# Graph network on one core: GpSimd's join to X moved into the second cell pass, biases added by one matmul per PSUM bank

## Time and profile before

| | us |
|---|---|
| median of 3 runs | 10096.06 |
| lowest, highest | 10090.6, 10096.87 |
| the profiled execution: its time | 10127.15 |
| its span, first to last instruction | 10125.4 |
| POOL busy in the span, share | 49% |
| PE, DVE, ACT busy | 55%, 52%, 46% |

### The profile page before, as it was taken

One profiled execution on the slowest core, in us unless ns is written; L12 is line 12 of the kernel. 1 busy time (PEld: TensorE's weight loads), 2 busy tenths in 40 slices (PEclk: granted clock), 3 DMA queues, 4 the chain that ended last, 5 costly groups with the idle time before them and its releaser, 6 DMA issues.

```text
span 10125.4 us, 129123 instructions
## 1 busy us (share of the span) xinstructions
PE 5609.1 (55%) x33883; PEld 4488.5 (44%) x33883; DVE 5300.4 (52%) x12476; ACT 4632.1 (46%) x8410; POOL 4936.4 (49%) x5153
## 2 busy tenths in 40 slices
PE   3999899734544545444455545544434444444446
PEld 2777666524444444443444444444423333333334
DVE  5888611335555555554555555555634444444445
ACT  2555300245555555553555555555434444444444
POOL 1000100356666666662566666666466666666660
PEclk9999899755555555555555555555555555555557
DMA  2333355134433434332344434443322222222221
GB/s 83 139 140 140 128 190 190 36 101 102 107 102 102 102 102 104 105 103 61 94 103 107 103 101 103 103 107 102 81 71 70 76 71 70 75 71 70 71 75 33
DMA packets 600502, 985.17 MB, mean 97 GB/s; under 512 B 330887, under 2 KB 454493, under 8 KB 560781
## 3 DMA queue, kind: packets, MB, share of 16 engines
q1 hardware_dynamic: 216924, 540.94, 16.1%
q0 software_dynamic: 163376, 356.21, 15.4%
q10 hardware_dynamic: 219648, 81.82, 3.0%
HBM read 755.78 MB, written 222.74 MB: 97 GB/s over the span
## 4 chain that ended last, share of the span: by engine, by line
PE 32%; DVE 21%; another core or an unknown queue 17%; DVEq 15%; issue 12%; ACT 1%; POOL 1%; POOLq 1%; DMA 0%; ACTq 0%; SPq 0%
PE bank L1038 12%; DVEq L1352 12%; DVE acc L1982 10%; PE bank L1264 9%; DVE arena L1969 3%; PE bank L1192 2%; PE bank L1062 2%; PE bank L1204 2%; DVEq L1982 2%; DVE bank L1938 2%; DVE arena L1940 1%; DVEq L1974 1%; DVE x_mem L1628 1%; PE bank L1174 1%
## 5 line engine op out<-in xcount | busy, mean ns | idle before, releaser
L704 POOL DMA_INDIRECT arena<-row_table,staged_idx x4980 | 4700.9, 944 | 3090.9 <-issue 1750.2
L1264 PE MATMUL bank<-arena 128*128 128x136 f32 x9984 | 2491.5, 430 | 1535.2 <-DVE acc L1982 739.9
L1264 PEld LDWEIGHTS bank<-arena 128*128 128x128 f32 x9984 | 2206.2, 317 | 1707.3 <-issue 1684.6
L1982 DVE TENSOR_TENSOR acc<-acc,bank 128x136 f32 x4992 | 1476.5, 296 | 2126.1 <-issue 822.6
L861 ACT ACTIVATE pick_dist<-col,dst_local 128x128 bf16<-128x128 f32 x4992 | 1521.8, 388 | 562.8 <-remote 492.0
L1038 PE MATMUL bank<-arena 128*128 128x385 bf16 (+1 forms) x7448 | 1324.8, 327 | 37.4 <-DVE arena L1722 20.9
L813 ACT COPY x_mem<-bank 128x384 f32<-128x384 f32 x416 | 198.9, 478 | 1813.1 <-remote 1159.1
L1038 PEld LDWEIGHTS bank<-arena 128*128 128x128 bf16 x7448 | 701.9, 98 | 458.5 <-issue 21.3
L648 POOL TENSOR_TENSOR arena<-acc,node_stat 128x896 f32 x14 | 23.9, 1709 | 1675.0 <-POOLq L660 988.0
L1969 DVE TENSOR_TENSOR arena<-arena,bank 128x528 f32<-128x528 f32 x1248 | 832.1, 687 | 0.7
L1204 PE MATMUL bank<-ident,x_mem 96*128 96x96 f32 x1664 | 364.7, 374 | 741.9 <-DVE x_mem L1630 574.4
(11 more groups left out here) (371 smaller groups left out, 5507.7 us busy)
## 6 DMA issues: line engine op xcount, KB each, us to landing
arena<-dst_rows SPq DMA_DIRECT2D x156, 1024.0 KB
cell_rows<-arena SPq DMA_DIRECT2D x75, 1568.0 KB, 5.1
arena<-cell_rows SPq DMA_DIRECT2D x75, 1568.0 KB, 6.6
edge_stats<-x_mem ACTq DMA_DIRECT2D x416, 192.0 KB
arena<-row_table,staged_idx POOLq DMA_INDIRECT x4980
x_mem<-in_edge_attr SPq DMA_DIRECT2D x208, 192.0 KB
x_mem<-segment_flags SPq DMA_DIRECT2D x416, 96.0 KB
arena<-change_rows SPq DMA_DIRECT2D x312, 64.0 KB
```

The source lines that it names most:

```text
L704: pool.indirect_dma_start(gathered[:, at, :], None, table, bass.IndirectOffsetOnAxis(staged_idx[:, at:at + 1], 0)).then_inc(att_gathered[n ...
L1264: mm = pe.matmul(region(k)[:, 0:ROW], pick[:, k, :], gathered[:, b * GROUP + k, :], start=True, stop=True)
L1982: done = dve.tensor_tensor(row, row, region(m * BATCH + k), ALU.add)
```

## The change

Two edits. On GpSimd, the additions of the parts of Hp and of gn_bias to X leave the loop with `scale_sums` and become a loop of their own, ahead of it, which waits only for d1.folded to be 2; the loop of `scale_sums` then waits for the end of the pass, as before. On PE, the bias matmul per tile becomes one matmul per PSUM bank with the bias broadcast over the tiles of that bank (512 and 384 columns for layer 1; 420, 420 and 140 for a table), and the accumulation is closed at the last tile of a bank.

```diff
             pool.memset(acc[:, :], 0.0).then_inc(n1.cleared, 1)
-            pool.wait_ge(d1.added, CG + 2)
-            pool.sem_inc(n2.turned, FREE)
+            pool.wait_ge(d1.folded, 2)
             with pool.Fori(0, NTG) as i:
-                scale_sums(n2, i)
-
                 x_group = X[:, bass.ds(i * TG, TG), :]
                 for m in range(PARTS):
                     pool.tensor_tensor(x_group, x_group, Hp[:, bass.ds(i * TG, TG), m * D:(m + 1) * D], ALU.add)
                     pool.drain()
                 pool.tensor_tensor(x_group, x_group, norm_par[:, 1, :].unsqueeze(1).to_broadcast([P, TG, D]),
                                    ALU.add).then_inc(n2.joined, 1)
+
+            pool.wait_ge(d1.added, CG + 2)
+            pool.sem_inc(n2.turned, FREE)
+            with pool.Fori(0, NTG) as i:
+                scale_sums(n2, i)
...
+                if bias is not None:
+                    for first in range(0, TG, 4):
+                        n = min(4, TG - first)
+                        pe.matmul(bank[:, 4 + first // 4, 0:n * P].rearrange("p (t w) -> p t w", w=P), part_ones[:, :],
+                                  bias.unsqueeze(1).to_broadcast([PARTS, n, P]), start=True, stop=False)
                 for t in range(TG):
-                    if bias is not None:
-                        pe.matmul(cols(4, t), part_ones[:, :], bias, start=True, stop=False)
                     pe.matmul(cols(4, t), own[:, t, :], w_own, start=bias is None, stop=False)
-                    mm = pe.matmul(cols(4, t), mean[:, t, :], w_mean, start=False, stop=True)
+                    mm = pe.matmul(cols(4, t), mean[:, t, :], w_mean, start=False,
+                                   stop=bias is None or t % 4 == 3 or t == TG - 1)
...
+                for first in range(0, TG, 3):
+                    tiles = min(3, TG - first)
+                    pe.matmul(bank[:, 2 + 3 * (i % 2) + first // 3, 0:tiles * TW].rearrange("p (t w) -> p t w", w=TW),
+                              part_ones[:, :], tab_bias[:, n, :].unsqueeze(1).to_broadcast([PARTS, tiles, TW]),
+                              start=True, stop=False)
                 for t in range(TG):
-                    pe.matmul(table_cols(i, t), part_ones[:, :], tab_bias[:, n, :], start=True, stop=False)
-                    mm = pe.matmul(table_cols(i, t), turned_own[i % 2][:, t, :], w_tab[:, n, :], start=False, stop=True)
+                    mm = pe.matmul(table_cols(i, t), turned_own[i % 2][:, t, :], w_tab[:, n, :], start=False,
+                                   stop=t % 3 == 2 or t == TG - 1)
```

## The result

The changed kernel takes 10032.44 us (median of 4 runs, 10027.24 to 10041.2), the kernel before on the same chip 10094.72 us (4 runs, 10090.6 to 10096.87). The ratio is 0.9945, 95% interval 0.9933 to 0.9957: 55 us by the ratio (43 to 68 by the interval), 62 us between the medians. Forecast were 10041 us and 55.5 us. In a second series on another chip the ratio was 0.9947 (0.9934 to 0.9961).

The account below looks back on a forecast made before the run. TensorE was taken to bound the second cell pass, GpSimd the product stage. Terms 31 + 7.5 + 15 + 10 - 8 = 55.5 us, off the median of 10096.06, gave 10041 us; range 10017 to 10074.

Parts of the forecast that it names:

- Join leaves the product stage: Layer 1's product stage: GpSimd's round shrinks to one multiplication, TensorE's idle 6.26 us goes; 31 us together with the bias.
- Bias, product stage: Layer 1's products: one bias matmul per bank saves net 2.0 us per group at full clock, within the stage's 31 us.
- Tables, first stage: First table stage: the first and last two product groups are on the path, 2.5 us each; gain 7.5 us.
- Tables, second stage: Second table stage: rounds fall from 8.45 to 6.50 us, then set by VectorE with ACT; gain 15 us.
- Tables, third stage: Third table stage: same code, with an unexplained 10.00 us ACT wait kept; gain 10 us, between 2.5 and 15.
- swallowed: Behind the table stages: if the "issue" wait ends at its own time, 32.5 us don't arrive; 10073 us, chance 0.11.
- Join in the pass: Start of the second pass: VectorE's small drained steps wait for GpSimd's moved join, the fold is late; loss 8 us.
- Let through: Start of the second pass: only VectorE steps with two SBUF inputs wait, fold in time; loss 0, 10033 us, chance 0.15.
- Starved: Start of the second pass: VectorE waits per instruction (10058 us) or until GpSimd's 28 are through (10083); chance 0.12.
- slower by the clock: Second pass: the new pause lowers TensorE's clock, 8.0 us per group; slower than before from seven groups; chance 0.05.

Follow-up runs that it names:

- late_join: Changed kernel, but GpSimd's join to X waits for VectorE's second fold (d1.folded 4 instead of 2); 10077.47 us, ratio 0.9940 to the kernel before.
- short_join: Changed kernel with each of GpSimd's 21 additions of Hp's parts cut in three; 10090.23 us in one run, kernel before 10148.3.
- pertile128: Kernel before with bias operands on 128 rows, still per tile, and the join to X behind VectorE's second fold; 10058.89 us, ratio 0.9938.
- rows128: Kernel before with bias operands on 128 rows instead of 3, zeros added; 10106.51 us in one run, later timed at 10084.08, ratio 0.9963.
- late128_tail: late_join with 128-row bias operands, the last 14 edge-sum gathers and their joining moved late into the third attention layer; 10051.72 us, ratio 0.9932 to before.

## Why the prediction was right, and where it wasn't

- **Join leaves the product stage**: right. Alone 17.2 us, with the bias 31.5; the next limit is TensorE with gelu, the round 6.40 us (6.15 said). The hit of half a us on the stage is partly luck: six rounds were 1.5 us longer in sum than said, and the last products, left wholly at the lower clock in the sum, fell to it only for a part of their time and were 1.6 us faster than that. In late_join, short_join and pertile128 they ran at full clock.
- **Bias, product stage**: the size was right, 1.8 us a group (2.0 said; 8.19 less 6.40), and the cause I gave was half wrong. I took 0.35 us as the matmul's slot. It is 0.11 us for the matmul and 0.24 for changing rows (rows128). The wide matmul wins by leaving one such change in a group instead of seven.
- **Tables, first stage**: right, 7.6 us.
- **Tables, second stage**: mechanism right, 15 us mis-sized. The round is VectorE's and ACT's, 6.50 us as said. But I left TensorE at half clock for its last two groups of products, 4.45 us each; they took 2.4, as its clock rose (0.95 in the last 7 us). The last copy gained 19.2 us in that profile and 17.7 in the second one, where one of the two groups took 4.05.
- **Tables, third stage**: the step that failed, though its sum came out near. I took the last row copy for the end of the path: it gained 23.7 us, not 10, and 8.7 arrived (18.0 and 7.0 in the second profile). That 10 and 8.7 lie near each other is luck. What I had not looked at was which queues the next layer starts from. GpSimd's 49 gathers outlast the table, so the layer's first gather is 9.6 us later behind the last copy (14.2 - 4.6); and VectorE's joining of the edge sums waits for the last of them and is over only 5.9 us ahead of the layer's first reduction. The "swallowed" rival was false for the second stage, where the chain still has one wait of 72.96 us behind the stage (73.24 before), and true by another mechanism for 15.0 of 23.7 us in the third.
- **Join in the pass**: right in place and mechanism, which late_join and short_join show, and 7.6 us of 8. That the fold came to 0.2 us is luck: the pass began 0.78 us earlier than in the trace that the sum used. The preparation took nine waits ahead of the fold, not eight. GpSimd started 0.36 us behind the clearing and not 0.6, so that the addition of L1731 (L1742 in the changed kernel) waited too; the one of L1743 (L1754) slipped through a gap; and L1764, three instructions, waited twice. The pause was 6.7 us instead of 5.2, the clock behind it 1.5 instead of 2.5, and the first 24 matmuls were 0.7 faster.
- **Let through**: false. L1746 and L1752 have a single SBUF input and took 1.7 and 1.8 us instead of 0.2. The Trainium skill's SBUF — State Buffer, section "Who interferes with whom", names casts and tensor_scalar among those that can use both ports, under conditions; the trace agrees with that part, as far as both waited, and with its rule that an instruction with two SBUF inputs waits (L1765, 1.72 us instead of 0.17). Which mode an instruction ran in no trace shows.
- **Starved**, **slower by the clock**: false. VectorE got a turn after each GpSimd instruction; after one group at 9.09 us the pass was back at 8.18.

The terms were off by 4.6 us (second table) and by 1.3 the other way (third), the others by half a us: 55.5 forecast, 59.8 by the stages of the first profile, 56 by those of the second, 55 by the ratio. What stays open is what the "remote" waits of 4 to 14 us in the third table stage are: they were there in every profile with gathers beside the stage and not in the one without; and whether the earlier start of layer 3 in late128_tail reaches its end.

## What to carry to other kernels

Count a stage's gain at the instruction that the next stage starts from, on each engine's queue, not at the stage's last one. When GpSimd's work moves beside VectorE's small drained steps, put it behind them, or cut it short: each step pays the rest of the running instruction. A matmul of 3 rows between ones of 128 cost more here for its shape than for its columns; give it the rows of its neighbours first.

## What the runs showed of the hardware

- A change of TensorE between 3 and 128 rows of operands and back cost 0.24 us at full clock and 0.31 at half; a bias matmul on 128 rows cost 0.11 at full clock (rows128 against the kernel before).
- With such changes in every tile of the second table stage TensorE stayed at 0.50 while it was busy for 56.5 of 57 us; with 128 rows in the same order of instructions it was at 0.90 in the last 34 us of that stage. In the product stage, with the same changes, the kernel before had 0.83.
- A VectorE step of 2 to 49 columns behind a drain that reads SBUF alone and starts beside a running GpSimd addition ends just behind it: it took 1.65 to 1.94 us beside additions of 1.81 to 2.08 us, and in short_join 0.45 to 0.93 us beside shorter ones, where a step of one column waited too. Steps that started in the gap of 0.15 to 0.23 us between two additions took 0.16 and 0.19 us (L1754, L1750). One with an input in PSUM kept its time beside a running addition (L1582, 0.42 us in both kernels).
